# First convolution fused with the transposition of the counts and the projections; out-degrees in the maxima stage

## The reference

```python
deg = maximum(segment_sum(ones, dst), 1);  deg_isqrt = deg ** -0.5
x = layernorm(x + L0(x, deg_isqrt, ...))     # relational convolution
x = layernorm(x + L1(x, ...))                # attention over the edges and self loops, 8 heads of 16
x = layernorm(x + L2(x, src, dst))           # feat * out_deg ** -0.5, sum over edges, @ weight, * in_deg ** -0.5
x = layernorm(x + L3(x, ...))                # two GCN convolutions with self loops

# L0
agg = segment_sum((h[src] + rel_emb[type]) @ W_neighbor, dst)
L0 = relu(agg * deg_isqrt + h @ loop_weight)
# L1
Q = relu(x @ query_kernel + query_bias);  K = relu(x @ key_kernel + key_bias);  V = x @ kernel
alpha = segment_softmax(sum(Q[row] * K[col], head), row)
L1 = segment_sum(alpha * V[col], row) + bias
```

## Time and profile before

| what | us |
|---|---|
| median of 3 runs | 2684.95 |
| the profiled execution, its own time | 2683.39 |
| its span, first to last instruction | 2681.6 |
| column sums (about 491 to 526.2) | 35 |
| first convolution, 526.2 to 665.3 | 139.1 |
| transposition and projections, 665.3 to 835.05 | 169.7 |
| maxima, 835 to 1560 | 725 |
| attention, 1560 to 2340 | 780 |
| the last two layers, 2340 to 2681.6 | 341.6 |

### The profile page before, as it was taken

The page is one execution under the profiler, slowest core; times in us unless marked ns, Lnnn a source line. Parts: engine busy times, 40 slices in busy tenths (PEclk is TensorE's granted clock), DMA queues, the critical chain, the costliest instruction groups (busy, mean ns, idle before and its releaser), DMA issues. The chain is left out here.

```text
span 2681.6 us, 40367 instructions
## 1 busy us (share of the span) xinstructions
PE 2230.7 (83%) x12449; PEld 959.8 (36%) x12520; DVE 2051.9 (77%) x2822; ACT 1150.4 (43%) x1435; POOL 80.2 (3%) x121
## 2 busy tenths in 40 slices
PE   1898898797775888888888868989889898699998
PEld 1555555354552222222222222222222222145555
DVE  4888787433444999999999979999999999843222
ACT  0777777355441110100101057879778787510000
POOL 0000000000001000000000000000000000121000
PEclk8999988899666999999999989999999999899999
DMA  1000000111665000000000034444444444300000
GB/s 44 1 0 0 0 0 0 44 49 41 197 228 172 6 9 6 9 6 6 9 6 9 3 99 118 115 108 120 112 118 115 112 115 112 86 8 1 1 9 17
DMA packets 283137, 148.01 MB, mean 55 GB/s; under 512 B 183150, under 2 KB 279020, under 8 KB 283013
## 3 DMA queue, kind: packets, MB, share of 16 engines
q1 hardware_dynamic: 283045, 146.79, 20.0%
HBM read 106.71 MB, written 41.63 MB: 55 GB/s over the span
## 5 line engine op out<-in xcount | busy, mean ns | idle before, releaser
L1379 DVE CUSTOM_DVE_ANT_0 ps<-ps,max_mask 128x1536 f32<-128x1536 f32 (+1 forms) x400 | 700.6, 1828 | 13.8 <-PE ps L1342 13.8
L1625 DVE SCALAR_TENSOR_TENSOR counts<-counts,att_a 128x1792 f32<-128x1792 f32 x263 | 517.4, 2019 | 38.4 <-ACT counts L1605 38.4
L1605 ACT ACTIVATE counts<-ps 128x896 f32<-128x896 f32 x526 | 454.1, 916 | 183.2 <-PE ps L1549 181.9
L1549 PE MATMUL ps<-att_q,att_k 99*128 99x448 bf16 x1400 | 339.3, 366 | 48.9 <-issue 23.2
L1367 ACT ACTIVATE max_mask<-counts 128x3136 uint8 x24 | 67.6, 2816 | 595.0 <-DVE max_mall L1387 595.0
L1558 PE MATMUL ps<-counts,att_v 128*32 128x448 f32 x2104 | 260.5, 568 | 36.7 <-DVE counts L1625 8.2
L467 ACT ACTIVATE counts<-ps 128x899 f32 x261 | 247.0, 946 | 99.2 <-PE ps L417 99.0
L1549 PEld LDWEIGHTS ps<-att_q,att_k 99*128 99x128 bf16 x1400 | 110.3, 99 | 381.6 <-issue 169.0
L1342 PE MATMUL ps<-counts,max_q 96*128 96x512 bf16 (+1 forms) x700 | 169.6, 359 | 79.9 <-DVE max_mx L1379 52.4
L413 PE MATMUL ps<-hot 128*128 128x192 bf16 (+1 forms) x474 | 201.7, 442 | 32.2 <-DVE hot L319 32.2
L909 PE MATMUL ps<-counts 128*128 128x512 bf16 (+1 forms) x1036 | 205.5, 358 | 20.9 <-POOL counts L936 20.2
(11 more groups left out here) (215 smaller groups left out, 2531.6 us busy)
## 6 DMA issues: line engine op xcount, KB each, us to landing
att_k<-keys SPq DMA_DIRECT2D x175, 198.0 KB
att_v<-values SPq DMA_DIRECT2D x175, 128.0 KB
counts_turned<-counts SPq DMA_DIRECT2D x25, 784.0 KB, 4.5
att_a<-counts_turned SPq DMA_DIRECT2D x175, 112.0 KB
max_q<-queries SPq DMA_DIRECT2D x25, 192.0 KB, 3.0
queries<-prj_pieces SPq DMA_DIRECT2D x42, 112.0 KB
keys<-prj_pieces SPq DMA_DIRECT2D x42, 112.0 KB
att_q<-queries SPq DMA_DIRECT2D x7, 519.8 KB
```

Of the source, the lines that this page charges most:

```text
L1379: v.tensor_tensor_reduce(out=flat[:, lo:hi], in0=flat[:, lo:hi], in1=mask[slot][:, lo:hi], scale=1.0, scalar=0.0, op0=ALU.mult, op1=ALU.ma ...
L1549: last = nc.tensor.matmul(m.bank[2 * (n % NS) + z][:, 0:CW], k[i][:, 2 * h + z, :], q[:, 2 * h + z, :], start=True, stop=True)
L1605: nc.scalar.activation(e[n % NE][:, :, :], m.ps[:, 2 * (n % NS):2 * (n % NS) + 2, 0:CW], ACT.Exp).then_inc(exped, 1)
L1625: v.scalar_tensor_tensor(w, w, 1.0, a[i % DG][:, :].unsqueeze(1).to_broadcast([P, 4, CW]), op0=ALU.min, op1=ALU.mult).then_inc(weighed, 1)
```

## The change

`graph_conv` and `turn_and_project` become one block, `first_layer`, without loops in the program (all is written out), over the seven chunks of whole blocks that the last stage already uses: four of 4 blocks (512 columns) and three of 3 (384). PE's list has eight rounds. Round c runs the 75 matmuls of chunk c in 25 steps of three; in round c, step u also carries what chunk c - 1 still needs: the transposition of its features at step 0, the products by both weights at 3, the transposition of its new features at 12, the query product at 14, the value product at 16, the key product at 17, and, from step 1 on, groups of up to four transposed blocks (28 groups for a chunk of 4, 21 for one of 3; in chunks of 4, two groups in each of steps 20 to 23). Round 0 has sums alone, round 7 the rest of the last chunk alone. Groups alternate between two PSUM banks; ACT copies all of them out, into three row buffers. The identity is added by POOL after a chunk's sums. DVE's list has the same steps. Out-degrees are summed by ACT in `score_maxima` (with the identity in the counts, so DVE subtracts 1), and their power is taken in the short block behind it. The powers of the in-degrees are taken at the start of `first_layer`. `column_sums` works in the same chunks, and drops its in-degrees.

```diff
+def first_layer(nc, m, ad, deg_d, aggr_d, x0, weight, loop_weight, wq, bq, wk, bk, wv, x1, qs, ks, vd):
...
+        NB = 3
+        rows = [m.spare[:, i * ND:(i + 1) * ND] for i in range(NB)]
...
+        bank_agg, bank_rows, bank_loop, bank_x, bank_qk, bank_turn = \
+            m.bank[0:2], m.bank[2], m.bank[3], m.bank[4], m.bank[5], m.bank[6:8]
+        NGR = -(-SB // 4)
...
+            for p in range(NCH):
+                lo, hi = FIRST[p], FIRST[p + 1]
+                if p + 1 < NCH:
+                    load_agg(p + 1)
+                store_turned(lo)
+                if p + 1 < NCH:
+                    load_rows(p + 1)
+                sp.wait_ge(finished, p + 1)
+                sp.dma_start(x1[lo * P:hi * P, :].rearrange("(b p) f -> p b f", p=P), y[:, 0:hi - lo, :])\
+                  .then_inc(x1_stored, 16)
+                store_turned(lo + 1)
+                store_cuts(p, 0, qs, Q_PIECES, q_cut, q_stored)
...
+                store_cuts(p, 1, ks, K_PIECES, k_cut, k_stored)
+                for i in range(lo + 2, hi):
+                    store_turned(i)
...
+            def turn(p, z):
+                n, i, g = group(p, z)
+                if z % NGR == 0:
+                    pe.wait_ge(looped, i + 1)
+                if n >= 2:
+                    pe.wait_ge(evac_act, n - 1)
+                for b in range(4 * g, min(4 * g + 4, SB)):
+                    last = nc.tensor.matmul(bank_turn[n % 2][:, (b - 4 * g) * P:(b - 4 * g + 1) * P],
+                                            m.at[:, b, i * P:(i + 1) * P], m.identb[:, :], start=True, stop=True)
+                last.then_inc(turned, 1)
...
+            def tasks(p, u):
...
+                elif u == 12:
+                    pe.wait_ge(finished, p + 1)
+                    for j in range(nb):
+                        last = nc.tensor.transpose(bank_x[:, j * P:(j + 1) * P], y[:, j, :], m.ident[:, :])
+                    last.then_inc(x1_turned, 1)
...
+            pe.wait_ge(w_loaded, 16 * 7)
+            for c in range(NCH + 1):
+                for u in range(SB):
+                    if c < NCH:
...
+                        for q in range(3):
+                            last = nc.tensor.matmul(bank_agg[c % 2][:, 0:n], pieces[:, q, u, :], m.at[:, u, at:at + n],
+                                                    start=u + q == 0, stop=q == 2 and u == SB - 1)
...
+                    if c:
+                        tasks(c - 1, u)
+                        for z in turns_at(c - 1, u):
+                            turn(c - 1, z)
+
+        def evacuate(eng, copy, done, p, z):
+            n, i, g = group(p, z)
+            if i >= NB:
+                eng.wait_ge(turned_stored[i % NB], 16 * (i // NB))
+            eng.wait_ge(turned, n + 1)
+            lo, hi = 4 * g, min(4 * g + 4, SB)
+            copy(rows[i % NB][:, lo * P:hi * P], bank_turn[n % 2][:, 0:(hi - lo) * P]).then_inc(done, 1)
...
 def score_maxima(nc, m, qs, ks):
...
+                    def degree(b, before):
+
+                        act.wait_ge(counted, before)
+                        nc.scalar.activation(junk[:, :], m.at[:, ds(b, 1), 0:NP].rearrange("p a n -> p (a n)"), ACT.Copy,
+                                             accum_out=m.out_norm[:, ds(b, 1)]).then_inc(counted, 1)
...
+                            degree(2 * i + z, 2 * i + z + 1)
...
-        graph_conv(nc, m, "L0", x0, None, L0_gnn_W_neighbor, m.in_norm, x1, residual=x0,
-                   loop_weight=L0_gnn_loop_weight, aggr_d=aggr_d, relu=True, out_degree=True)
-        turn_and_project(nc, m, ad, deg_d, x1, L1_gnn_query_kernel, L1_gnn_query_bias, L1_gnn_key_kernel,
-                         L1_gnn_key_bias, L1_gnn_kernel, qs, ks, vd)
+        first_layer(nc, m, ad, deg_d, aggr_d, x0, L0_gnn_W_neighbor, L0_gnn_loop_weight, L1_gnn_query_kernel,
+                    L1_gnn_query_bias, L1_gnn_key_kernel, L1_gnn_key_bias, L1_gnn_kernel, x1, qs, ks, vd)
```

More of the change, by code:

```diff
@@ L488, in split3 @@
     s.link(v.tensor_tensor(parts[2], x, parts[1], op=ALU.subtract))
+CHUNKS = (4, 4, 4, 4, 3, 3, 3)
+NCH = len(CHUNKS)
+FIRST = tuple(sum(CHUNKS[:c]) for c in range(NCH + 1))
 def column_sums(nc, m, t, rel, aggr_d, deg_d):
@@ L534, in _ @@
             pe.wait_ge(filled, 1)
-            for c in range(NC):
+            for c in range(NCH):
                 if c >= 2:
@@ L538, in _ @@
                 for b in range(TB):
-                    last = nc.tensor.matmul(m.bank[2 + c % 2][0:1, 0:CW], ones[:, 0:1],
-                                            t.rt[:, b, c * CW:(c + 1) * CW], start=b == 0, stop=b == TB - 1)
+                    last = nc.tensor.matmul(m.bank[2 + c % 2][0:1, 0:size[c]], ones[:, 0:1],
+                                            t.rt[:, b, cols[c]], start=b == 0, stop=b == TB - 1)
                 last.then_inc(counted, 1)
             pe.wait_ge(step, 4)
-            for c in range(NC):
+            for c in range(NCH):
                 if c >= 2:
@@ L825 @@
-CHUNKS = (4, 4, 4, 4, 3, 3, 3)
-NCH = len(CHUNKS)
-FIRST = tuple(sum(CHUNKS[:c]) for c in range(NCH + 1))
 def conv_chain(nc, m, x2, w2, w3a, b3a, w3b, b3b, out):
@@ L1145, in _ @@
+            sp.wait_ge(x1_stored, 16 * NCH)
+            sp.wait_ge(q_stored, 16 * NX * NCH)
+            sp.wait_ge(k_stored, 16 * NX * NCH)
+            sp.wait_ge(v_stored, 16 * NCH)
+            sp.wait_ge(ones_stored, 16)
+            for i in range(NB):
+                sp.wait_ge(turned_stored[i], 16 * len(range(i, SB, NB)))
         @block.tensor
         def _(pe):
[L1148 to L1160 removed]
@@ L1276, in _ @@
-            over_chunks(v, body)
+            v.memset(ones, 1.0).then_inc(ones_filled, 1)
+            for c in range(NCH):
+                lo, hi = FIRST[c], FIRST[c + 1]
+                t = raw[c % NB][:, 0:hi - lo, :]
+                v.wait_ge(first_piece, c + 1)
+                v.tensor_tensor(t, t, pieces[:, 0, lo:hi, :], op=ALU.subtract).then_inc(cut, 1)
+                v.wait_ge(second_piece, c + 1)
+                v.tensor_tensor(pieces[:, 2, lo:hi, :], t, pieces[:, 1, lo:hi, :], op=ALU.subtract)\
+                 .then_inc(pieces_ready, 1)
```

673 lines of the change are left out of this document (274 added, 399 removed).

## The result

The changed kernel takes 2577.85 us (median of 4 runs, 2575.87 to 2583.13), the kernel before, beside it, 2684.28: a ratio of 0.9607, 95% interval 0.9591 to 0.9624. The profiled execution took 2577.15 us, span 2575.4, 106.2 us less than the one of before. Nearly all of it is gone from the two stages that became one: 308.9 us before, 202.9 now, from the first load at 524.96 to the next stage's at 727.82. The maxima stage is within 1 us as long as it was.

What follows compares the result with a forecast made beforehand. Two old stages, 308.9 us, were taken as bounded by round trips; the new stage, summed by TensorE's work, waits and last round, saves 95.7 us, so 2683.39 - 95.5 = 2587.9, left at 2588; range 2574 to 2622, forecast's own 2575 to 2600.

Steps and rivals of the forecast that it cites:

- degrees free: Maxima stage: ScalarE's 25 out-degree sums of 2.8 us lie in its idle time; counted 0, up to 70 us otherwise.
- the last round: Round without sums to cover it, ended by SP's stores: 25 us, bounds 20 and 30.
- Bounded by round trips, not by an engine: Old convolution and transposition, 308.9 us: TensorE and the copying engine take turns, each standing still half of the time.
- rounds 1 to 6: Sums of one chunk plus the previous chunk's remaining work, priced on TensorE at the full clock: 154.0 us together.
- met waits: New loop: 230 waits of TensorE cost 33 ns each even when met, 7.6 us; between 0 and twice that.
- fp32 work: Per block in the rounds: two transposes, three products, share of query and key products, 1.44 us.
- Start: New stage starts at 526.5 us; the first matmul waits for seven small loads, until 533.3.
- the three powers at the end: GpSimd's three powers of 4.33 us ending the old transposition stage, counted as part of the 95.7 us gain.
- Clock low: Rival: TensorE's clock stays low in rounds 1 to 6; 2742 us if throughout, 2% for over 62%, 4% in part.
- Late stores: Rival: stores of turned rows land late, stalling ScalarE, then TensorE, in six rounds: +27 us, 2615; 12%.
- Late chain: Rival: VectorE's chain from products to normalized rows comes 2.5 us later, past its margin: 8 us, 2596; 12%.
- ScalarE's pace: Rival: ScalarE's copies take 1 us each and pace the loop: +30 us, 2618; 3%.

Runs made afterwards that it cites:

- bunched: Changed kernel with all groups of a chunk behind the last sum of a round, not one by one between sums: 2658.6 us.
- bunched_filled: The bunched kernel with one useless matmul of 512 columns more behind each group, to keep TensorE busy: 2641.65 us.
- no_degrees: Changed kernel without the 25 out-degree sums in the maxima stage, degrees set to a constant: 2578.3 us.
- early_last: Changed kernel with TensorE's wait for weights moved to round 1, second power behind chunk 0's loops, last stores reordered over two queues: 2573.8 us.
- before_powers_early: Kernel before the change, with all three degree powers at the start of the transposition stage, not its end: 2684.2 us.

## Why the prediction was right, step by step

2588 was forecast, 2577.85 measured, 10 us below it, inside the forecast's own range (2575 to 2600). The mechanism held: rounds bounded by TensorE at the full clock, ScalarE and the stores hidden, degrees free. That the time lies inside that range is in part luck: the range varied the waits and the last round alone, and a price that it held fixed was too high by some 6 us, while the last round went the other way.

- **Where the gain comes from.** "Bounded by round trips, not by an engine" is shown by three kernels. Before to bunched is -25 us: one pass in place of two, written out, and still standing in line. Bunched to bunched_filled is -17, the clock; from there to the changed kernel -64, evacuations beside sums, or in the last chunk beside fp32 products. What makes up the 25 is only argued: the idle 14.89 us of TensorE at the seam of the two stages are gone, and so are the groups at 126 ns a matmul. The 1.35 us that ScalarE's copy waits in the earlier trace rows are in the main such a group: eight matmuls of 126 ns are 1.0 us.
- **The mis-sized term: rounds 1 to 6**, 154.0 + 7.6 us forecast, 149.7 measured (551.01 to 700.75). Two prices were too high. A turning matmul costs 52 to 58 ns, not 66, so 550 of them some 6 us less: I divided 1.06 us by 16, but a merged row carries 0.17 us of its last matmul's end. Four take 0.39 and eight 0.61 us in these traces, so each more takes 55 ns, and (1.06 - 0.17)/16 is the same 55. A sum costs 0.2155, not 0.219, for the same reason. And the 7.6 us for met waits, taken from the attention, are no more than 0.6 us in a full round: a wait that was met long ago, behind other matmuls, costs next to nothing.
- **fp32 work:** a full round without turns is 21.93 us, less 75 x 0.2155 = 5.8 us for four blocks, the 4 x 1.44 that were forecast.
- **Start:** forecast 526.5, here 524.96; the kernels above with the same column sums start from 525.49 to 526.77, so this looks like scatter. From there to the end of round 0 26.0 us, forecast 25.9.
- **The last round** is 27.1 us for 25.3. SP's stores at its end came as forecast, but TensorE's last groups wait for ScalarE, and query pieces are stored at 13.3 us and not at 12.5; the next stage's load comes 4.9 us after the last row is issued.
- **Unforeseen:** 1.2 us in round 1, where the second power (4.33 us) holds up GpSimd's loops: the two powers did not lie in round 0. The wait varies (2.6 us in no_degrees, which has the same first stage); early_last has none. And 1.0 us behind the stage, 0.9 of it in the maxima (715.8 us from the first load to the last maximum, 714.9 before). The degree sums are not all of it, if any (715.5 without them); the rest is open.
- **A wrong reading:** the three powers at the end, which my text counted as part of the gain, were none; with all three at its start the old stage takes as long (before_powers_early). No term of the sum used them.
- **Rivals.** Clock low: 1.00 in all six rounds; it fell where the groups stood in a bunch. Late stores: ScalarE waits 1.1 us for them in all, but one buffer less costs 22.5, so the case was near. Late chain: in round 1 normalized rows were ready with 1.3 us to spare, and TensorE never waited for them longer than 0.5 (0.7 in all). ScalarE's pace: 0.55 us per copy back to back, never the bound.

The Trainium skill's 81 ns for the small matmul ("TensorE: Matmul & The Clock Gate", section "Back-to-back issue gap") is further off than my 66. The same section's formula for a single matmul, N/2.4 + 2.5 ns, gives 56 for 128 columns and 216 for 512. The trace has 55 and 215.5 in a sustained stream.

## What to carry to other kernels

When two engines hand small groups to and fro, put the groups one by one between long work that waits for nobody: the same evacuations then cost next to nothing, where in bunches standing in line for them cost 64 us here. A low clock beside short waits is a sign to look for the round trip; raising the clock alone gave nothing in the old stage. Before pricing the clock, look whether the groups on the path speed up with it: at 1.00 and at 0.50, those behind a wait kept the same pace there. Take the price of a repeated instruction from starts, or from the difference of two merged rows, not from one row's length over its count.

## What the runs showed of the hardware

- In this profile a row of 128-column matmuls at the full clock holds 0.17 us that are no part of the pace: 0.39 us for four, 0.61 for eight, 55 ns for each more.
- In the old loop, with a register instruction ahead of each small matmul, groups that begin on a wait took 126 ns a matmul at a granted clock of 1.00 as at 0.50. In the written-out kernels such groups took 59 ns at 1.00 and 98 at 0.50.
- Filling matmuls raise the granted clock (0.63 to 0.95 in the kernel before, 0.73 to 1.00 in a bunch). The first gave no time that could be told, the second 17 us.
- Stores issued from a second queue shared the time: nine stores of pieces took 4.88 + 3.87 us on SP's queue, beside 4.30 for three on ScalarE's.
